# Gram's attention, its query block: three product banks, one bank pair for turning, totals a tile ahead, copies by ScalarE alone, first contexts normalised between the tiles

## The chip, the cores and the metric

The kernel runs on one core of a Trainium2 chip. The metric is the device time of one execution in microseconds. TensorE is the matrix engine, VectorE (DVE) and ScalarE (ACT) are the two that read its results from PSUM, GpSimd (POOL) works on SBUF alone here, and SyncE (SP) issues the transfers.

## The reference

Four layers of gated cross-attention and feed-forward over 32 sequences of 56 tokens of width 128, each attending to a context of 1500 rows. The change is in the attention of the third layer (`L2_xattn`), 16 heads of 64, which has no softmax:

```python
Qn = _layernorm(Q, ln1_g, ln1_b)
Kn = _layernorm(K, ln1_g, ln1_b)
Vn = _layernorm(V, ln1_g, ln1_b)
q = _split_heads(Qn @ wq, B, Nq)
k = _split_heads(Kn @ wk, B, Nk)
v = _split_heads(Vn @ wv, B, Nk)
qn = _l2norm(q)      # q / max(sqrt(sum(q * q)), 1e-12), per head
kn = _l2norm(k)
attn = jnp.einsum('bhqd,bhkd->bhqk', qn, kn)
out = jnp.einsum('bhqk,bhkd->bhqd', attn, v)
x = Q + out @ wo + bo
```

Since nothing nonlinear stands between the two products, the kernel never forms `attn`: it sums a Gram matrix of normalised keys and contexts for each sequence and multiplies the queries into it.

## The kernel before

`attention2` computes this layer with queues written out by hand: each engine has its list of instructions, in the order of the code, and semaphores between them. It has three blocks with a barrier between each. The block `attn2q`, the one that changes, makes the normalised queries of all 1792 tokens, in 16 tiles (`TILES`) of 112 tokens (`PAIR`, two sequences). The block `attn2k` behind it goes over the 32 sequences with their contexts, in 12 chunks of 125 rows (`CH`, `KC`); it needs the queries, turned, and the first sequence's context, normalised. The block `attn2m` is the layer's small network.

In `attn2q`, TensorE first multiplies the value and output weights of each head (`vo`, into the two product banks `pq[0]` and `pq[1]`, each two PSUM banks of 512 columns); ScalarE copies them to `w_vo`. Each tile t then goes these ways:

- *query*: TensorE, two products of 512 columns each (L2282; each shows as two passes in the trace), into `pq[t % 2]`;
- *square*: ScalarE, 112x1024, into `q_sq` (L2306);
- *total*: VectorE sums the squares by head (L2327); *root*: ScalarE (L2309);
- *clip* and *reciprocal*: VectorE, 112x16 (L2332, L2333); then `qn`: VectorE scales the product bank by them (L2335), which also frees the bank;
- *turning*: TensorE transposes `qn` in eight pieces (L2273) into `pt[t % 2]`, a pair of PSUM banks; *copy*: ScalarE takes one bank (L2300), VectorE the other (L2323), into `q_t`.

TensorE's queue goes query(0), query(1), turning(0), query(2), turning(1) and so on. Query(t) waits for `qn`(t-2), because of its bank. ScalarE's goes square(t), root(t), copy(t-1); VectorE's total(t), copy(t-1), clip(t), reciprocal(t), `qn`(t).

The first sequence's context is normalised beside this: its statistics by VectorE ahead of tile 0 (`context_stats`, `context_scales`), a root by ScalarE (`context_root`, L2229), the twelve chunks by ScalarE (`context_normed`, L2235), gain and shift by GpSimd over all twelve in two instructions (`context_affine`, L2240 and L2243), which wait for the last chunk. For the other sequences the same happens in `attn2k`.

All eight PSUM banks are taken in this block: four by `pq`, four by `pt`.

## Time and profile before

| | us |
|---|---|
| median of three runs | 6049.69 |
| lowest, highest | 6029.98, 6051.38 |
| profiled execution, its time | 6069.86 |
| profiled execution, its span | 6067.9 |
| TensorE busy in it | 5280.6 (87%) |
| VectorE busy | 4463.5 (74%) |
| ScalarE busy | 3193.1 (53%) |
| GpSimd busy | 1846.4 (30%) |
| mean granted TensorE clock | 0.94 of 2.4 GHz |

The span is from the first to the last instruction of the execution that was profiled; its time is 2 us more. All rows below are of this one execution, and times in them count from its start. Busy time is that of an engine's own instructions. A row in order of time gives the start, the duration, the engine and the line, then output, inputs and shapes; behind it in brackets stands how long the engine had been idle and what ended that.

### The profile page before, as it was taken

What the parts mean: (1) busy time and instruction counts of PE and PEld (TensorE: products, weight loads), DVE (VectorE), ACT (ScalarE), POOL (GpSimd) and SP (SyncE); (2) the same over time, 40 slices, a digit from 0 to 9 for tenths busy, and PEclk for the clock granted to TensorE, in tenths of its full rate; (3) what the DMA queues carried; (4) which work ended last, traced back from release to release, by engine and by line L of the source; (5) the groups of instructions that cost most, each with busy time, mean ns of one, the idle gap of its engine ahead of it and who ended that gap; (6) DMA issues with size and microseconds to landing.
All of it is one profiled execution on the core that took longest, in us unless ns stands there. A gap on an engine that the chain in (4) does not pass through costs nothing. (4 is left out here: it accounts for less than half of the span.)

```text
span 6067.9 us, 133226 instructions
## 1 busy us (share of the span) xinstructions
PE 5280.6 (87%) x51447; PEld 3803.5 (63%) x51447; DVE 4463.5 (74%) x9176; ACT 3193.1 (53%) x6024; POOL 1846.4 (30%) x1447
## 2 busy tenths in 40 slices
PE   3898898988679999987949999999999749999997
PEld 1777777777268887865924444444444427878885
DVE  7888888886367777762457777777777557777776
ACT  1666666666256666642224444444444326666663
POOL 5776767672122222202021111111111022222220
PEclk6999999999789999988979999999999879999998
DMA  5655555553267777742010000000000049888891
GB/s 126 132 122 131 126 128 126 126 128 80 51 128 140 139 135 142 141 84 101 22 33 26 16 15 15 15 15 15 15 15 10 8 101 156 159 163 162 161 156 28
DMA packets 369568, 545.00 MB, mean 90 GB/s; under 512 B 116084, under 2 KB 248310, under 8 KB 368806
## 3 DMA queue, kind: packets, MB, share of 16 engines
q1 hardware_dynamic: 366982, 533.81, 43.5%
q8 instruction: 380, 6.23, 0.5%
q0 software_dynamic: 2048, 3.67, 0.2%
q14 instruction: 158, 1.29, 0.1%
HBM read 413.45 MB, written 123.90 MB: 89 GB/s over the span
## 5 line engine op out<-in xcount | busy, mean ns | idle before, releaser
L698 DVE CUSTOM_DVE_ANT_0 attn_logits<-attn_scores,attn_shift 112x750 f32<-112x750 f32 x1024 | 945.8, 933 | 436.5 <-PE attn_scores L503 436.5
L616 ACT ACTIVATE attn_probs_t<-attn_pt 125x448 f32<-125x448 f32 x1536 | 829.4, 541 | 583.7 <-PE attn_pt L518 563.2
L518 PEld LDWEIGHTS attn_pt<-ident,attn_logits 112*125 112x125 f32 x6144 | 852.6, 189 | 180.0 <-issue 95.1
L518 PE MATMUL attn_pt<-ident,attn_logits 112*125 112x112 f32 x6144 | 921.4, 273 | 26.7 <-ACT attn_logits L607 23.8
L2385 PE MATMUL attn2k_pk<-attn_wk,attn_cn_t 128*125 128x512 f32 x1536 | 740.1, 604 | 39.8 <-ACT attn_cn_t L2451 36.6
L2396 PE MATMUL attn2k_pg<-attn_kn,attn_cn 125*128 125x512 f32 x1536 | 726.2, 595 | 4.5 <-ACT attn_gram L2459 2.3
L2504 DVE TENSOR_REDUCE attn_ss<-attn_sq 125x16 f32<-125x1024 f32 x384 | 467.0, 1216 | 245.3 <-ACT attn_sq L2478 245.0
L415 POOL CAST attn_k_parts<-xn_t 128x500 bf16<-128x500 f32 x192 | 206.3, 1075 | 1429.2 <-DVE xn_t L670 1429.2
L2478 ACT ACTIVATE attn_sq<-attn2k_pk 125x1024 f32<-125x1024 f32 x384 | 391.5, 1019 | 330.8 <-PE attn2k_pk L2385 330.6
L1230 ACT ACTIVATE attn_probs_t<-attn_pt 125x448 f32<-125x448 f32 x768 | 413.9, 539 | 278.2 <-PE attn_pt L1117 276.3
L2385 PEld LDWEIGHTS attn2k_pk<-attn_wk,attn_cn_t 128*125 128x125 f32 x1536 | 274.7, 187 | 400.6 <-issue 298.3
L503 PE MATMUL attn_scores<-attn_k_packed,attn_q_blocks 96*112 96x375 bf16 x2048 | 515.2, 333 | 9.9 <-DMA attn_k_packed<-k_scratch 8.2
L2516 DVE TENSOR_TENSOR attn_kn<-attn2k_pk,attn_rn 125x1024 f32<-125x1024 f32 x384 | 470.2, 1224 | 13.4 <-DVE attn_rn L2513 0.2
L1105 PE MATMUL attn_scores<-attn_k_packed,attn_q_blocks 96*112 96x375 bf16 x1024 | 353.3, 345 | 125.6 <-DVE attn_tops L1411 125.5
L2396 PEld LDWEIGHTS attn2k_pg<-attn_kn,attn_cn 125*128 125x128 f32 x1536 | 264.6, 192 | 299.0 <-issue 287.2
L1411 DVE CUSTOM_DVE_ANT_0 attn_logits<-attn_scores,attn_bias,attn_floor 112x750 f32<-112x750 f32 x342 | 338.2, 989 | 96.9 <-PE attn_scores L1107 95.2
L2367 POOL COPY attn_q_now<-attn_q_t 128x448 f32 (+1 forms) x32 | 17.8, 556 | 1194.2 <-PE attn2k_pz L2417 1135.3
L1219 ACT ACTIVATE attn_logits<-attn_logits,attn_neg_top 112x750 f32<-112x750 f32 x342 | 313.1, 916 | 102.3 <-DVE attn_neg_top L1419 100.1
L607 ACT ACTIVATE attn_logits<-attn_logits,attn_neg_top 112x750 f32<-112x750 f32 x384 | 351.3, 915 | 3.9 <-DVE attn_neg_top L706 0.6
L531 PE MATMUL attn_po<-attn_probs_t,attn_v 125*32 125x112 f32 x12288 | 347.9, 261 | 1.5 <-ACT attn_probs_t L616 1.3
L1107 PE MATMUL attn_scores<-attn_masked,attn_pusher 112*112 112x375 bf16 x1024 | 341.3, 333 | 0.0
L452 PE MATMUL attn_side<-attn_ctx_t,attn_wk 128*128 128x500 f32 x376 | 207.8, 635 | 147.1 <-DVE xn_t L670 77.1
(371 smaller groups left out, 10444.3 us busy)
## 6 DMA issues: line engine op xcount, KB each, us to landing
attn_k_packed<-k_scratch SPq DMA_DIRECT2D x372, 375.0 KB
attn_k_packed<-k_scratch SPq DMA_DIRECT2D x408, 187.5 KB, 4.4
k_scratch<-attn_k_parts SPq DMA_DIRECT2D x64, 1125.0 KB
attn_ctx_t<-in_ctx_t SPq DMA_DIRECT2D x64, 750.0 KB
k_scratch<-attn_k_parts SPq DMA_DIRECT2D x96, 375.0 KB, 3.7
attn_ctx_t<-in_ctx_t SPq DMA_DIRECT2D x96, 250.0 KB, 4.6
attn_ctx<-in_ctx SPq DMA_DIRECT2D x32, 750.0 KB
attn_mask_in<-in_mask SPq DMA_DIRECT2D x192, 109.4 KB
```

What stands on the lines that cost most here:

```text
L503: last = pe.matmul(scores[h][0:PAIR, b, 0:QTR], q_blocks[:, n % 2, p, :, :].rearrange("p a s -> p (a s)"), k_packed[:, n % 2, p, h * HALF ...
L518: last = pe.transpose(pt[(3 * at + t) % 2][0:KC, (c % 4) * PAIR:(c % 4 + 1) * PAIR], logits[:, at % 3, c * KC:(c + 1) * KC], g.ident[0:PAI ...
L607: act.activation(at, at, ACT.Identity, bias=neg_top[:, n % 2, p:p + 1]).then_inc(act_lowered, 1)
L616: act.activation(probs_t[0:KC, p // 4, 4 * t:4 * t + 4, (p % 4) * PAIR:(p % 4 + 1) * PAIR], pt[(3 * at + t) % 2][0:KC, 0:QUAD].rearrange(" ...
L698: dve.tensor_tensor_reduce(out=logits[:, at % 3, cols].rearrange("p (b k) -> p b k", b=2), in0=scores[h][0:PAIR, :, 0:QTR], in1=shift[:, n ...
L1105: pe.matmul(scores[h][0:PAIR, b, 0:QTR], q_blocks[:, n % 2, p, :, :].rearrange("p a s -> p (a s)"), k_packed[:, at % KEY_RING, cols], star ...
L1230: act.activation(probs_t[0:KC, at % PV_RING, 4 * t:4 * t + 4, :], pt[(3 * at + t) % 2][0:KC, 0:QUAD].rearrange("p (c q) -> p c q", c=4), A ...
L2385: last = pe.matmul(pk[c % 2][0:KC, b, :], cn_t[:, c % 2, :], wk[:, b * HW:(b + 1) * HW], start=True, stop=True)
L2396: last = pe.matmul(pg[:, b, :], cn[:, j, c, :], kn[:, c % 2, b * HW:(b + 1) * HW], start=(c == 0), stop=(c == CH - 1))
L2478: act.activation(sq[:, c % 2, :].rearrange("p (a b) -> p a b", a=2), pk[c % 2][0:KC, :, :], ACT.Square).then_inc(sq_ready, 1)
L2504: dve.tensor_reduce(ss[:, c % 2, :], sq[:, c % 2, :].rearrange("p (h d) -> p h d", h=H2), AX.X, ALU.add).then_inc(ss_ready, 1)
L2516: dve.tensor_tensor(kn[:, c % 2, :].rearrange("p (h d) -> p h d", h=H2), pk[c % 2][0:KC, :, :].rearrange("p a (h d) -> p (a h) d", h=8), r ...
```

## The change

Three pairs of PSUM banks for products instead of two, and one pair for turning instead of two. TensorE makes three queries ahead and then, behind the turning of tile t, the query of tile t+3; a turning waits for the copy of the tile before. ScalarE copies the weights first, works on squares two tiles and roots one tile ahead, copies both banks of a turned tile in one instruction, and normalises one chunk of the first context behind each of the copies 0 to 11. VectorE copies nothing and makes the total of a tile before it normalises the tile ahead of it.

```diff
--- before.py
+++ after.py
@@ -2245,11 +2245,11 @@
 
         r = scope(nc, "attn2q")
         with r.ctx:
-            pq = [r.ps(f"pq{i}", [128, 2, 512]) for i in range(2)]
-            pt = [r.ps(f"pt{i}", [128, 2, 512]) for i in range(2)]
-            vo_ready, vo_copied, q_ready, q_sq_ready, q_ss_ready, q_root_ready, q_steps, qn_ready, q_turned, act_copied, dve_copied = (
+            pq = [r.ps(f"pq{i}", [128, 2, 512]) for i in range(3)]
+            pt = r.ps("pt", [128, 2, 512])
+            vo_ready, vo_copied, q_ready, q_sq_ready, q_ss_ready, q_root_ready, q_steps, qn_ready, q_turned, copied = (
                 r.sem(n) for n in ("vo_ready", "vo_copied", "q_ready", "sq_ready", "ss_ready",
-                                   "root_ready", "steps", "qn_ready", "q_turned", "act_copied", "dve_copied"))
+                                   "root_ready", "steps", "qn_ready", "q_turned", "copied"))
             with nc.Block() as block:
                 @block.gpsimd
                 def _(pool):
@@ -2267,49 +2267,62 @@
 
                     def turn(t):
                         pe.wait_ge(qn_ready, t + 1)
-                        wait(pe, act_copied, t - 1)
-                        wait(pe, dve_copied, t - 1)
+                        wait(pe, copied, t)
                         for p in range(HP):
-                            last = pe.transpose(pt[t % 2][:, p // 4, (p % 4) * PAIR:(p % 4 + 1) * PAIR],
+                            last = pe.transpose(pt[:, p // 4, (p % 4) * PAIR:(p % 4 + 1) * PAIR],
                                                 qn[:, t % 2, p * 128:(p + 1) * 128], g.ident[0:PAIR, 0:PAIR])
                         last.then_inc(q_turned, 1)
 
-                    for t in range(TILES):
+                    def query(t):
                         if t < 2:
                             pe.wait_ge(vo_copied, t + 1)
-                        wait(pe, qn_ready, t - 1)
+                        wait(pe, qn_ready, t - 2)
                         for c in range(2):
-                            last = pe.matmul(pq[t % 2][0:PAIR, c, :], g.z_t[:, t * PAIR:(t + 1) * PAIR],
+                            last = pe.matmul(pq[t % 3][0:PAIR, c, :], g.z_t[:, t * PAIR:(t + 1) * PAIR],
                                              wq[:, c * HW:(c + 1) * HW], start=True, stop=True)
                         last.then_inc(q_ready, 1)
-                        if t:
-                            turn(t - 1)
-                    turn(TILES - 1)
+
+                    for t in range(3):
+                        query(t)
+                    for t in range(TILES):
+                        turn(t)
+                        if t + 3 < TILES:
+                            query(t + 3)
 
                 @block.scalar
                 def _(act):
-                    context_root(act, 0)
-                    context_normed(act, 0, 0, range(CH))
                     for half in range(2):
                         act.wait_ge(vo_ready, half + 1)
                         act.activation(w_vo[:, 8 * half:8 * half + 8, :].rearrange("p h d -> p (h d)"),
                                        pq[half][:].rearrange("p a b -> p (a b)"), ACT.Copy).then_inc(vo_copied, 1)
 
+                    def square(t):
+                        act.wait_ge(q_ready, t + 1)
+                        wait(act, q_ss_ready, t - 1)
+                        act.activation(q_sq[:, t % 2, :].rearrange("p (a b) -> p a b", a=2), pq[t % 3][0:PAIR, :, :],
+                                       ACT.Square).then_inc(q_sq_ready, 1)
+
+                    def root(t):
+                        act.wait_ge(q_ss_ready, t + 1)
+                        act.activation(q_ss[:, t % 2, :], q_ss[:, t % 2, :], ACT.Sqrt).then_inc(q_root_ready, 1)
+
                     def copy(t):
                         act.wait_ge(q_turned, t + 1)
-                        act.activation(q_t[:, 0:4, t * PAIR:(t + 1) * PAIR],
-                                       pt[t % 2][:, 0, 0:QUAD].rearrange("p (a b) -> p a b", a=4),
-                                       ACT.Copy).then_inc(act_copied, 1)
+                        act.activation(q_t[:, :, t * PAIR:(t + 1) * PAIR].rearrange("p (g a) b -> p g a b", g=2),
+                                       pt[:, :, 0:QUAD].rearrange("p g (a b) -> p g a b", a=4),
+                                       ACT.Copy).then_inc(copied, 1)
+                    context_root(act, 0)
+                    square(0)
+                    square(1)
+                    root(0)
                     for t in range(TILES):
-                        act.wait_ge(q_ready, t + 1)
-                        wait(act, q_ss_ready, t - 1)
-                        act.activation(q_sq[:, t % 2, :].rearrange("p (a b) -> p a b", a=2), pq[t % 2][0:PAIR, :, :],
-                                       ACT.Square).then_inc(q_sq_ready, 1)
-                        act.wait_ge(q_ss_ready, t + 1)
-                        act.activation(q_ss[:, t % 2, :], q_ss[:, t % 2, :], ACT.Sqrt).then_inc(q_root_ready, 1)
-                        if t:
-                            copy(t - 1)
-                    copy(TILES - 1)
+                        if t + 2 < TILES:
+                            square(t + 2)
+                        if t + 1 < TILES:
+                            root(t + 1)
+                        copy(t)
+                        if t < CH:
+                            context_normed(act, 0, 0, (t,))
 
                 @block.vector
                 def _(dve):
@@ -2318,25 +2331,23 @@
                     context_scales(dve, 0)
                     chain = Chain(dve, q_steps)
 
-                    def copy(t):
-                        dve.wait_ge(q_turned, t + 1)
-                        dve.tensor_copy(q_t[:, 4:8, t * PAIR:(t + 1) * PAIR],
-                                        pt[t % 2][:, 1, 0:QUAD].rearrange("p (a b) -> p a b", a=4)).then_inc(dve_copied, 1)
-                    for t in range(TILES):
+                    def total(t):
                         dve.wait_ge(q_sq_ready, t + 1)
                         dve.tensor_reduce(q_ss[:, t % 2, :], q_sq[:, t % 2, :].rearrange("p (h d) -> p h d", h=H2),
                                           AX.X, ALU.add).then_inc(q_ss_ready, 1)
-                        if t:
-                            copy(t - 1)
+
+                    total(0)
+                    for t in range(TILES):
+                        if t + 1 < TILES:
+                            total(t + 1)
                         dve.wait_ge(q_root_ready, t + 1)
                         chain(dve.tensor_scalar(q_rn[:, t % 2, :], q_ss[:, t % 2, :], 1e-12, None, ALU.max))
                         chain(dve.reciprocal(q_rn[:, t % 2, :], q_rn[:, t % 2, :]))
                         wait(dve, q_turned, t - 1)
                         dve.tensor_tensor(qn[:, t % 2, :].rearrange("p (h d) -> p h d", h=H2),
-                                          pq[t % 2][0:PAIR, :, :].rearrange("p a (h d) -> p (a h) d", h=8),
+                                          pq[t % 3][0:PAIR, :, :].rearrange("p a (h d) -> p (a h) d", h=8),
                                           q_rn[:, t % 2, :].unsqueeze(2).broadcast_to((PAIR, H2, DH2)),
                                           ALU.mult).then_inc(qn_ready, 1)
-                    copy(TILES - 1)
 
         r = scope(nc, "attn2k")
         with r.ctx:
```

The first place is TensorE's queue from the block's start. `attn2q_pq` are the product banks, `attn2q_pt` the banks for turning; L2264 makes the weight products, `x4` are two queries of two instructions each. Before:

```order
L2259 UNCONDITIONAL_BRANCH
L2264 MATMUL attn2q_pq<-attn_wo,attn_wv_t 128x128 x16
L2282 MATMUL attn2q_pq<-attn_wq,z_t 112x512 x4
L2273 MATMUL attn2q_pt<-ident,attn_q_qn 128x112 x8
L2282 MATMUL attn2q_pq<-attn_wq,z_t 112x512 x2
```

And now:

```order
L2259 UNCONDITIONAL_BRANCH
L2264 MATMUL attn2q_pq<-attn_wo,attn_wv_t 128x128 x16
L2281 MATMUL attn2q_pq<-attn_wq,z_t 112x512 x6
L2272 MATMUL attn2q_pt<-ident,attn_q_qn 128x112 x8
L2281 MATMUL attn2q_pq<-attn_wq,z_t 112x512 x2
```

Three queries instead of two stand ahead of the first turning; from there on one turning and one query alternate in both.

The second place is ScalarE's queue from the block's start. Before:

```order
L2229 ACTIVATE attn_var<-attn_var 125x12
L2235 ACTIVATE attn_cn<-attn_ctx,attn_off,attn_rs 125x128 x12
L2295 ACTIVATE attn_w_vo<-attn2q_pq 128x1024 x2
L2306 ACTIVATE attn_q_sq<-attn2q_pq 112x1024
L2309 ACTIVATE attn_q_ss<-attn_q_ss 112x16
L2306 ACTIVATE attn_q_sq<-attn2q_pq 112x1024
L2309 ACTIVATE attn_q_ss<-attn_q_ss 112x16
L2300 ACTIVATE attn_q_t<-attn2q_pt 128x4x112
```

And now:

```order
L2296 ACTIVATE attn_w_vo<-attn2q_pq 128x1024 x2
L2229 ACTIVATE attn_var<-attn_var 125x12
L2302 ACTIVATE attn_q_sq<-attn2q_pq 112x1024 x2
L2307 ACTIVATE attn_q_ss<-attn_q_ss 112x16
L2302 ACTIVATE attn_q_sq<-attn2q_pq 112x1024
L2307 ACTIVATE attn_q_ss<-attn_q_ss 112x16
L2311 ACTIVATE attn_q_t<-attn2q_pt 128x8x112
L2235 ACTIVATE attn_cn<-attn_ctx,attn_off,attn_rs 125x128
```

The weight copies (`attn_w_vo`) moved ahead of everything, the twelve contexts (`attn_cn`) stand one by one behind the copies of tiles 0 to 11, squares run two tiles ahead and roots one, and a copy takes all eight pairs of heads.

The third place is VectorE's queue at its first tiles, behind the statistics of the first sequence. Before:

```order
L2327 TENSOR_REDUCE attn_q_ss<-attn_q_sq 112x16
L2332 TENSOR_SCALAR attn_q_rn<-attn_q_ss 112x16
L2333 RECIPROCAL attn_q_rn<-attn_q_rn 112x16
L2335 TENSOR_TENSOR attn_q_qn<-attn2q_pq,attn_q_rn 112x1024
L2327 TENSOR_REDUCE attn_q_ss<-attn_q_sq 112x16
L2323 COPY attn_q_t<-attn2q_pt 128x4x112
L2332 TENSOR_SCALAR attn_q_rn<-attn_q_ss 112x16
```

And now:

```order
L2336 TENSOR_REDUCE attn_q_ss<-attn_q_sq 112x16 x2
L2344 TENSOR_SCALAR attn_q_rn<-attn_q_ss 112x16
L2345 RECIPROCAL attn_q_rn<-attn_q_rn 112x16
L2347 TENSOR_TENSOR attn_q_qn<-attn2q_pq,attn_q_rn 112x1024
L2336 TENSOR_REDUCE attn_q_ss<-attn_q_sq 112x16
```

The copy is gone from this queue, and between two normalisations stands the total of the tile after the next one (before: of the next one).

## Rows read from the trace of the kernel before

**Rows 1.** The page, its first lines: span, and busy time of the engines.
```profile
span 6067.9 us, 133226 instructions
...
PE 5280.6 (87%) x51447; PEld 3803.5 (63%) x51447; DVE 4463.5 (74%) x9176; ACT 3193.1 (53%) x6024; POOL 1846.4 (30%) x1447
```

**Rows 2.** Windows: stretch, length, busy PE, PEld, DVE, ACT, POOL, clock, DMA, GB/s.
```profile
3126.60:3182.80 56.20, 40.75 (x181) 20.30 (x179) 49.96 (x75) 25.55 (x45) 2.84 (x1) 1.00 0.00 1
3182.80:3185.00 2.20, 0.00 (x0) 0.00 (x0) 2.13 (x5) 0.65 (x2) 0.00 (x0) 0.86 0.00 0
3185.00:3188.00 3.00, 1.75 (x8) 1.41 (x8) 0.69 (x2) 0.54 (x1) 0.00 (x0) 0.50 0.00 0
3188.00:3200.00 12.00, 8.41 (x11) 2.95 (x11) 3.68 (x9) 2.87 (x6) 0.55 (x1) 0.58 0.30 91
```

**Rows 3.** Waits in 3123 to 3188: who for whom, us, times, longest.
```profile
PE attn2q_pt L2273 <- DVE attn_q_qn L2335: 17.8, 16, 2.7
DVE attn_q_ss L2327 <- ACT attn_q_sq L2306: 13.9, 8, 10.3
ACT attn_q_sq L2306 <- PE attn2q_pq L2282: 11.9, 15, 2.7
```

**Rows 4.** Order of time, two tiles and the end: start, duration, engine.
```profile
3177.89 0.99 PE L2273 MATMUL attn2q_pt<-ident,attn_q_qn 112*128 112x112 f32 x8 [0.63 <-DVE attn_q_qn L2335]
...
3178.71 1.88 PE L2282 MATMUL attn2q_pq<-attn_wq,z_t 128*112 128x512 f32 x4
...
3180.51 1.22 DVE L2335 TENSOR_TENSOR attn_q_qn<-attn2q_pq,attn_q_rn 112x1024 f32<-112x1024 f32 x1
3180.63 1.02 ACT L2306 ACTIVATE attn_q_sq<-attn2q_pq 112x1024 f32<-112x1024 f32 x1 [0.38 <-PE attn2q_pq L2282]
3181.69 1.22 DVE L2327 TENSOR_REDUCE attn_q_ss<-attn_q_sq 112x16 f32<-112x1024 f32 x1
...
3182.82 0.61 DVE L2323 COPY attn_q_t<-attn2q_pt 128x448 f32<-128x448 f32 x1
3182.94 0.21 ACT L2309 ACTIVATE attn_q_ss<-attn_q_ss 112x16 f32<-112x16 f32 x1 [1.29 <-DVE attn_q_ss L2327]
...
3183.35 0.17 DVE L2332 TENSOR_SCALAR attn_q_rn<-attn_q_ss 112x16 f32<-112x16 f32 x1
...
3183.84 1.23 DVE L2335 TENSOR_TENSOR attn_q_qn<-attn2q_pq,attn_q_rn 112x1024 f32<-112x1024 f32 x1
...
3185.12 1.75 PE L2273 MATMUL attn2q_pt<-ident,attn_q_qn 112*128 112x112 f32 x8 [2.35 <-DVE attn_q_qn L2335]
...
3186.91 0.63 DVE L2323 COPY attn_q_t<-attn2q_pt 128x448 f32<-128x448 f32 x1 [1.85 <-PE attn2q_pt L2273]
```

**Rows 5.** Order of time at the block's start.
```profile
3113.21 7.16 PE L2264 MATMUL attn2q_pq<-attn_wo,attn_wv_t 64*128 64x128 f32 x32 [1.82 <-PEq L105]
...
3117.63 4.72 ACT L2235 ACTIVATE attn_cn<-attn_ctx,attn_off,attn_rs 125x128 f32<-125x128 f32 x12 [0.50 <-DVE attn_off L2225]
3122.26 1.91 ACT L2295 ACTIVATE attn_w_vo<-attn2q_pq 128x1024 f32<-128x1024 f32 x2
...
3123.31 5.18 PE L2282 MATMUL attn2q_pq<-attn_wq,z_t 128*112 128x512 f32 x8 [2.94 <-ACT attn_w_vo L2295]
...
3126.82 1.02 ACT L2306 ACTIVATE attn_q_sq<-attn2q_pq 112x1024 f32<-112x1024 f32 x1 [2.65 <-PE attn2q_pq L2282]
...
3129.87 1.22 DVE L2335 TENSOR_TENSOR attn_q_qn<-attn2q_pq,attn_q_rn 112x1024 f32<-112x1024 f32 x1
```

**Rows 6.** Groups in 3120 to 3188: ScalarE's copy of a turned half.
```profile
L2300 ACT ACTIVATE attn_q_t<-attn2q_pt 128x448 f32<-128x448 f32 x16 | 8.4, 526 | 3.3 <-PE attn2q_pt L2273 3.3
```

**Rows 7.** The block behind: GpSimd and VectorE in time, and line 2511.
```profile
3229.12 3.44 POOL L2240 TENSOR_TENSOR attn_cn<-attn_cn,attn_gain 125x1536 f32<-125x1536 f32 x1 [40.25 <-ACT attn_cn L2235]
...
3231.48 1.11 DVE L2511 TENSOR_SCALAR attn_rn<-attn_ss 125x16 f32<-125x16 f32 x1 [0.28 <-ACT attn_ss L2483]
...
L2511 DVE TENSOR_SCALAR attn_rn<-attn_ss x384: 155/175/1112, 3198.3 to 4757.1; 125x16 f32<-125x16 f32 x192
```

## The prediction

> **What bounds the kernel now.** I began with the page: TensorE is busy for 87% of a span of 6067.9 us, VectorE for 74% [rows 1]. Those are averages over eight layers, and the change touches one block of one layer, so I went on to the table of windows around that block. It runs from 3113.2 to 3187.5 us: some 74 us, 1.2% of the span. In the stretch 3126.60 to 3182.80 VectorE is busy for 49.96 of 56.20 us and TensorE for 40.75, at a granted clock of 1.00 (2.4 GHz) [rows 2]. So VectorE is nearly, not wholly, the bound, and the waits say why. VectorE's `total` waits for ScalarE's `square` eight times, in every other tile; `square` waits for the query product in 15 tiles; TensorE's turning waits 17.8 us in all for `qn` [rows 3]. (10.3 of VectorE's 13.9 us is the first wait, ahead of tile 0.) A ring of three engines sets the pace.
>
> The order of time gives the ring's length [rows 4]. From the start of one turning to that of the next but one, start to start: turning to query 0.82 us; query to square 1.92; square to total 1.06; total to VectorE's copy 1.13; copy to clip 0.53; clip to `qn`, with the reciprocal between, 0.49; `qn` to turning 1.28. Sum 7.23, and that is what lies between the first and the last of these rows (3177.89 to 3185.12) for two tiles. The query behind the turning of tile t is that of tile t+2, hence two tiles a lap: 3.62 us a tile.
>
> **The change, part by part.**
>
> VectorE's copy goes. It stands in the ring with 0.53. The new ring is: turn(t), then query(t+3), square(t+3), total(t+3), and since totals are now a tile ahead, total(t+3) stands directly before clip(t+2), `qn`(t+2), which turn(t+2) waits for. The third product bank lets the query run three tiles ahead, but the total, a tile ahead too, takes that tile back: a lap is still two tiles. Its length is 0.82 + 1.92 + 1.06 + 1.13 + 0.49 + 1.28 = 6.70 us, 3.35 a tile. The root of tile t+2 was taken a tile earlier, so clip doesn't wait for it. VectorE by itself needs 1.13 + 0.49 + 1.18 (`qn` to the next total, 3180.51 to 3181.69 [rows 4]) = 2.80, so tiles come by turns after 2.80 and 3.90 us. From `qn`(0) to `qn`(14) there are seven laps, 46.90 us. `qn`(15) has no total ahead of it and follows 1.18 + 0.49 = 1.67 us later: 48.57. Before, it took from 3129.87 [rows 5] to 3183.84 [rows 4], 53.97. **Gain 5.4.**
>
> ScalarE's copy grows from 448 to 896 columns. 448 take 0.526 us [rows 6], two of 1024 columns take 1.91 [rows 5], about 1.00 each, so 896 take between 0.53 and 1.05 (twice the half copy). I take 0.90, the line between 526 and 1003 ns. With one bank for turning, turn(t+1) waits for copy(t): turning 0.98, copy 0.90 and two hops of 0.04 make 1.96 us after the turning began, and the next `qn` is ready 2.80 after it at the earliest. So the lost second bank costs nothing while TensorE has its fast clock; 0.84 us of cover is left. ScalarE's other work in a tile: square 1.02 and root 0.21 [rows 4], one context 0.39 (12 in 4.72 [rows 5]); with the copy 2.5 of at least 2.80. The context stands behind the copy: turning to end of copy 1.96, plus 0.39 is 2.35, and the next square can start only 0.82 + 1.92 = 2.74 after the turning. It hides, with 0.4 to spare; without that cover it would cost its 12 x 0.39 = 4.7.
>
> The head. Before, ScalarE normalises 12 contexts (4.72) ahead of the two weight copies, and TensorE's query waits for them until 3123.31, though its products ended at 3120.37 [rows 5]. Now the first weight copy starts when its products are there, the second from 3120.41 to 3121.4 under query(0), so query(0) starts at about 3120.40. The eight passes of the first two queries take 5.18 with the clock as it then rises [rows 5]; I keep 5.18, so square(1) starts at 3125.62. `qn`(0) now stands behind total(1): + 1.06 + 1.13 + 0.49 = 3128.30. **Gain 1.57** against 3129.87: of the 2.9 us that the query starts earlier, the second tile's total takes 1.3 back.
>
> The tail. `qn`(15) starts at 3128.30 + 48.57 = 3176.87, `qn`(14) at 3175.20, turn(14) at 3176.48. TensorE's last query is now behind turn(12), so before turn(14) it has been idle for some 2.9 us. Before, the granted clock was 0.86 in the 2.20 us stretch ahead of the last turning and 0.50 in the one that holds it, and that turning took 1.75 us instead of 0.98 [rows 2, 4]. I give turn(14) and turn(15) 1.75 each: turn(14) to 3178.23, copy 0.90, turn(15) 3179.2 to 3180.97, copy to 3181.90. That is 5.03 after `qn`(15) began, where before it was 3.70 (3183.84 to 3187.54). **Loss 1.33.**
>
> GpSimd's two instructions on the contexts (3.44 us each) move from the head, where VectorE had nothing to do, to the middle of the loop: context 11 is done at about 3168.2, so they lie at 3168.4 to 3171.8 and 3171.9 to 3175.3, 6 us before the block's end. They are hidden from the next block, but not from VectorE: while a GpSimd instruction ran from 3229.12 to 3232.56, a small TENSOR_SCALAR of VectorE started at 3231.48 and took 1.11 us, to that very end; the median of 384 of them is 175 ns [rows 7]. clip is such an instruction. clip(13), due at 3170.8, would be held to 3171.8, which the 1.10 us of slack before the next long tile absorbs; clip(14), due at 3174.7, to 3175.3, less its own 0.17. **Loss 0.4.** The Trainium skill says so too ("SBUF — State Buffer", section "Who interferes with whom"): the two engines share a port pair, locked for the whole instruction, which a tensor_scalar can take and a tensor_reduce never does; by that rule the hold is the whole rest of GpSimd's instruction. By this rule, the trace agrees (1.11 us, to the instruction's end), and taken alone it allows two full holds, 6.5 us.
>
> Sum: 5.40 + 1.57 - 1.33 - 0.4 = 5.2 us. The profiled execution (6069.86) would become 6064.7; it lies 20 us above the median of the three runs, 6049.69, but the block's waits are a matter of engines and hold for both, so I take the difference off the median: **6044.5**. What comes behind the block is unchanged and merely starts earlier: its 12 us under a clock of 0.58 [rows 2] follow an idle TensorE before and now. That is the largest unknown: with 8.41 us of products in it, a full clock would save 4.2, and a stay at half speed as much longer would cost about 4.
>
> **The rivals.**
>
> *VectorE sets the pace* (0.08). If squares come early enough in each tile, only 2.80 a tile is left: 14 x 2.80 + 1.67 = 40.9 instead of 48.57, and 6037. For it: the third bank. Against it: the query is still issued behind the turning that waits for `qn`.
>
> *The loop's gain is eaten* (0.17). Place: VectorE's clip under GpSimd's pass over the contexts. Two full holds cost 2 x (3.44 - 0.17) = 6.5, giving 6050.7. For it: the hold in [rows 7]. Against it: the clips are due late in GpSimd's instructions, and half of it falls into slack. The same time comes out if the contexts do not hide on ScalarE (4.7, 6049). It would decide from a hold of 5 us on.
>
> *Slower: TensorE runs the loop at half clock* (0.05). A query then takes 3.47 (that of tile 0, 3123.31 to the square's 3126.82 [rows 5]) and a turning 1.75, 5.22 a tile on TensorE alone: from 3120.4 on 83.5 and a copy, to 3204.8 instead of 3187.5, so 17 us slower, 6067. It decides if the idle before a turning in the loop grows from 1.2 us to the length that went ahead of the fall at the end, near 2. In the new ring it is 3.90 - 2.70 (0.82 and the query's 1.88) = 1.20 at most, as now, so I don't expect it.
>
> **How the numbers follow.** 30 us are what this kernel's measurement tells from no change (0.5%), 40% of the whole block; no case here reaches it. Forecast 0.70 (6044.5, with its unknowns 6040 to 6049), rivals 0.30; what lies beyond all is the program's own scatter, 21 us over three runs. Range: 6037 on the near side and 6051 on the far one, each carried 6 to 11 us further for that scatter of a median: 6026 to 6057. Faster by over 0.5% 0.03, within 0.5% 0.94, slower 0.03.
>
> **What would show it.** In the profile after: `qn` starts by turns 2.8 and 3.9 us apart (steps of 2.8 throughout: the first rival; near 5: the third); VectorE waits for square in every other tile, about 1.1 us; the first query starts within 0.1 us of the last weight product; ScalarE's 896 columns near 0.90; one or two clips of 0.5 to 1.1 us; the last two turnings at 1.75; the block ends near 69 us after its first product instead of 74.3. The prediction is wrong if the block gains over 10 us or nothing, or if the next block's first 12 us change length.

## The result: slower by 0.56%

The changed kernel takes 6075.71 us (median of 6 runs, 6071.14 to 6088.99), the kernel before 6047.57 in its six. The ratio is 1.0056, with a 95% interval of 1.0039 to 1.0074: slower, where no change that can be measured was forecast, and 19 us beyond the far end of the range.

The profiled execution took 6088.99 us. Its page has these lines for [rows 1]:

```profile
span 6087.1 us, 133211 instructions
PE 5304.3 (87%) x51447; PEld 3808.0 (63%) x51447; DVE 4456.8 (73%) x9160; ACT 3200.4 (53%) x6024; POOL 1847.6 (30%) x1447
q14 instruction: 223, 1.83, 0.1%
```

The last line had no part in the prediction; in the page of before it reads:

```profile
q14 instruction: 158, 1.29, 0.1%
```

The queue that brings the engines' code moves 65 packets of 8 KB more, for a program that is 15 instructions shorter (16 fewer of VectorE, one more of TensorE).

**The query block is faster.** This is the changed kernel in order of time: the block's first product, the first queries and `qn`s, two turns of the loop, and the end.

```profile
3096.15 7.16 PE L2264 MATMUL attn2q_pq<-attn_wo,attn_wv_t 64*128 64x128 f32 x32 [1.81 <-PEq L105]
...
3103.24 7.72 PE L2281 MATMUL attn2q_pq<-attn_wq,z_t 128*112 128x512 f32 x12
...
3109.28 1.02 ACT L2302 ACTIVATE attn_q_sq<-attn2q_pq 112x1024 f32<-112x1024 f32 x1 [1.23 <-PE attn2q_pq L2281]
...
3111.96 1.22 DVE L2347 TENSOR_TENSOR attn_q_qn<-attn2q_pq,attn_q_rn 112x1024 f32<-112x1024 f32 x1
...
3114.27 0.92 ACT L2311 ACTIVATE attn_q_t<-attn2q_pt 128x896 f32<-128x896 f32 x1 [2.14 <-PE attn2q_pt L2272]
...
3114.72 1.23 DVE L2347 TENSOR_TENSOR attn_q_qn<-attn2q_pq,attn_q_rn 112x1024 f32<-112x1024 f32 x1
...
3117.05 1.22 DVE L2336 TENSOR_REDUCE attn_q_ss<-attn_q_sq 112x16 f32<-112x1024 f32 x1 [1.11 <-ACT attn_q_sq L2302]
...
3118.67 1.22 DVE L2347 TENSOR_TENSOR attn_q_qn<-attn2q_pq,attn_q_rn 112x1024 f32<-112x1024 f32 x1
...
3121.43 1.23 DVE L2347 TENSOR_TENSOR attn_q_qn<-attn2q_pq,attn_q_rn 112x1024 f32<-112x1024 f32 x1
...
3152.12 3.44 POOL L2240 TENSOR_TENSOR attn_cn<-attn_cn,attn_gain 125x1536 f32<-125x1536 f32 x1 [90.77 <-ACT attn_cn L2235]
...
3154.59 1.01 DVE L2344 TENSOR_SCALAR attn_q_rn<-attn_q_ss 112x16 f32<-112x16 f32 x1
...
3155.65 3.44 POOL L2243 TENSOR_TENSOR attn_cn<-attn_cn,attn_shift 125x1536 f32<-125x1536 f32 x1
...
3158.39 0.73 DVE L2344 TENSOR_SCALAR attn_q_rn<-attn_q_ss 112x16 f32<-112x16 f32 x1
...
3160.72 1.76 PE L2272 MATMUL attn2q_pt<-ident,attn_q_qn 112*128 112x112 f32 x8 [2.54 <-DVE attn_q_qn L2347]
...
3161.07 1.22 DVE L2347 TENSOR_TENSOR attn_q_qn<-attn2q_pq,attn_q_rn 112x1024 f32<-112x1024 f32 x1
...
3165.34 0.92 ACT L2311 ACTIVATE attn_q_t<-attn2q_pt 128x896 f32<-128x896 f32 x1 [1.91 <-PE attn2q_pt L2272]
```

`qn` starts by turns 2.76 and 3.95 us apart (3111.96, 3114.72, 3118.67, 3121.43). From the first product to the last copy's end it is 3166.26 - 3096.15 = 70.1 us, against 3187.54 - 3113.21 = 74.3 [rows 4, 5]: 4.2 us less, where 5.2 were forecast.

**The block behind it is slower.** Here every key product of the following block (`attn2k_pk`) as one group, first in the kernel before, then in the changed one; the last two times are the first and the last start:

```profile
L2385 PE MATMUL attn2k_pk<-attn_wk,attn_cn_t x1536: 590/592/1218, 3189.1 to 4753.9; 128*125 128x512 f32 x192
```

```profile
L2396 PE MATMUL attn2k_pk<-attn_wk,attn_cn_t x1536: 590/592/1216, 3167.8 to 4774.7; 128*125 128x512 f32 x192
```

1564.8 us have become 1606.9. The same products are made by the same lines, and their durations are the same; 42.1 us have come in between them. The waits of the changed kernel from 3167 to 4779 us name the place:

```profile
DVE attn_ss L2515 <- ACT attn_sq L2489: 230.3, 238, 10.4
...
DVE attn_ss L2515 <- issue: 55.5, 13, 4.6
```

"Issue" is time in which an engine waited for nothing that the profile shows. Before, VectorE has no such wait in this stretch. There are 13 of 4.1 to 4.6 us, and each stands at the same place: where VectorE's hardware loop over the sequences (`sequences`, 14 passes of two sequences each) jumps back to its start. One in VectorE's order of time, then the same place in the kernel before:

```profile
3466.70 1.23 DVE L2527 TENSOR_TENSOR attn_kn<-attn2k_pk,attn_rn 125x1024 f32<-125x1024 f32 x1
3472.05 1.22 DVE L2515 TENSOR_REDUCE attn_ss<-attn_sq 125x16 f32<-125x1024 f32 x1 [4.13 <-issue]
3473.19 0.86 DVE L2207 BATCH_NORM_STATS2 attn_stats<-attn_ctx 125x6 f32<-125x128 f32 x4
```

```profile
3484.30 1.23 DVE L2516 TENSOR_TENSOR attn_kn<-attn2k_pk,attn_rn 125x1024 f32<-125x1024 f32 x1
3487.36 1.22 DVE L2504 TENSOR_REDUCE attn_ss<-attn_sq 125x16 f32<-125x1024 f32 x1 [1.84 <-ACT attn_sq L2478]
3488.50 0.86 DVE L2207 BATCH_NORM_STATS2 attn_stats<-attn_ctx 125x6 f32<-125x128 f32 x4
```

Before, the pause is 1.84 us and ends with ScalarE's square. After, it is 4.13, nothing in the program ends it, and a pass takes 101.2 us on average instead of 98.0. In the 7 us around it (3466 to 3473) the only transfers in the whole core are these:

```profile
DMA packets 3, 0.02 MB, mean 4 GB/s; under 512 B 0, under 2 KB 0, under 8 KB 0
## 3 DMA queue, kind: packets, MB, share of 16 engines
q14 instruction: 3, 0.02, 1.2%
```

Three packets of code, the first just as the normalisation ends, the next two 2.4 us apart. 65 packets more are 13 times 5: five for each repeated pass.

The spans add up. Ahead of the query block the changed kernel's profile is 17.1 us shorter (3096.15 against 3113.21), in code that the change leaves alone. What makes that difference was not settled: some waits there are shorter (VectorE's for `ffn_silu`, 158.7 us against 177.9), others longer (for `ffn_py`, 74.0 against 57.4). Over the kernels below the query block begins at 3079 to 3132 us, and the repeated times of one kernel spread over 15 to 32 us. Then -4.2 in the query block, +42.1 in the key products, -1.6 behind them: +19.2, the difference of the spans (6087.1 and 6067.9). Of the medians' 28 us, the two blocks give +38; the rest is within that scatter.

### The profile page after: what moved, and what is told of

It reads as the page before. It is cut to its first block and busy times, and to the rows that moved or that the text cites. A ratio compares the mean times of both kernels' runs of the same rounds, so it can differ in the third digit from the quotient of the medians.

```text
span 6087.1 us, 133211 instructions
## 1 busy us (share of the span) xinstructions
PE 5304.3 (87%) x51447; PEld 3808.0 (63%) x51447; DVE 4456.8 (73%) x9160; ACT 3200.4 (53%) x6024; POOL 1847.6 (30%) x1447
## 5 line engine op out<-in xcount | busy, mean ns | idle before, releaser
L2515 DVE TENSOR_REDUCE attn_ss<-attn_sq 125x16 f32<-125x1024 f32 x384 | 467.1, 1216 | 287.6 <-ACT attn_sq L2489 230.3
L2494 ACT ACTIVATE attn_ss<-attn_ss 125x16 f32<-125x16 f32 x384 | 82.8, 216 | 511.4 <-DVE attn_ss L2515 511.4
```

What stands on the lines that cost most here:

```text
L2515: dve.tensor_reduce(ss[:, c % 2, :], sq[:, c % 2, :].rearrange("p (h d) -> p h d", h=H2), AX.X, ALU.add).then_inc(ss_ready, 1)
```

## The experiments

What could make VectorE fetch code in its loop? Counted in the built program, its stream has 9777 instructions before and 9761 after (the 16 copies are gone), and the loop's body, 288 instructions long, starts at number 6757 before and 6741 after. The four streams other than TensorE's hold 20388 instructions before; over 158 packets that is 129 for a packet of 8 KB. If code lies in pieces of 128, as this suggests, a body of 288 lies in three pieces, unless it starts in the last 31 places of one; then it lies in four. That is the **theory of place**: sixteen instructions fewer ahead of the loop moved its head to the end of a piece. Its rivals: the **new order** of the query block leaves engines or data in a state that slows what follows; or the **execution** itself, a disturbance that would come with any program.

Most kernels here differ from the changed one by one edit, in `attention2`, with N and the place varied. The increments are of a semaphore that nobody waits for, and leave the computation as it is:

```
                         qn(t)
+                    for _ in range(N):
+                        dve.sem_inc(held, 1)
```

**pad16**: N = 16, behind the last `qn` of the query block. It keeps all that the change does and puts the loop's head back to where it was.

> The changed kernel with 16 semaphore increments of VectorE, which nobody waits for, behind its last qn in the query block. They change nothing but the place of what follows in VectorE's instruction stream: the loop of 14 passes in the block behind stands where it stood in the kernel before (the change took 16 copies out of that stream ahead of it). Theory P (place of the code): the 13 stalls of 4.1 to 4.6 us at the head of VectorE's loop body go, as do the 65 extra packets of the instruction queue (158 packets again), the block behind takes 1568 us again instead of 1611, and the kernel takes 6043 +- 6 us, 0.1% under the kernel before; the query block stays at 70 us. Theory B (the block's new order puts the engines into another step with each other, and the loop behind runs slower for it): the increments change no order, so the stalls stay and the time stays at 6076. Theory D (the slow loop is a matter of the execution, not of the program): times of both kinds, 6043 and 6080, among the runs.

Ratio to the kernel before 0.9993 (0.9976 to 1.0009), and on its page and in its trace:

```profile
q14 instruction: 158, 1.29, 0.1%
```

```profile
L2398 PE MATMUL attn2k_pk<-attn_wk,attn_cn_t x1536: 590/592/1217, 3182.2 to 4745.6; 128*125 128x512 f32 x192
```

1563.4 us for the key products, no wait on "issue" in VectorE, and a query block of 70.8 us. Sixteen instructions more take the loss away.

**pad16_behind**: the same sixteen, put behind VectorE's loop.

> The same 16 increments, but behind VectorE's loop instead of ahead of it. Theory P: the loop stands where it stands in the changed kernel, so nothing is cured: 13 stalls, 223 packets of the instruction queue, 6076 +- 6 us. Theory B: 6076 as well. If some 16 increments anywhere cure it (the length of the program, not the loop's place), 6043.

1.0045 (1.0032 to 1.0058); 223 packets, 13 waits on "issue" (54.4 us in all), key products 1601.0 us. It has as many instructions as pad16, and the median is 33 us longer (6099.51 and 6066.28, on one chip). So it is what stands ahead of the loop that counts.

**act_copies**: the kernel before, in its old order, with only the copies given to ScalarE. VectorE's stream is shorter by the same sixteen.

```
-                        wait(pe, dve_copied, t - 1)
...
-                        act.activation(q_t[:, 0:4, t * PAIR:(t + 1) * PAIR],
-                                       pt[t % 2][:, 0, 0:QUAD].rearrange("p (a b) -> p a b", a=4),
+                        act.activation(q_t[:, :, t * PAIR:(t + 1) * PAIR].rearrange("p (g a) b -> p g a b", g=2),
+                                       pt[t % 2][:, :, 0:QUAD].rearrange("p g (a b) -> p g a b", a=4),
...
-                        if t:
-                            copy(t - 1)
...
-                    copy(TILES - 1)
```

> The kernel before with one part of the change alone: ScalarE copies both halves of a turned tile (896 columns), VectorE none; two product banks, two for turning, the old order of everything else. VectorE's stream ahead of the loop loses the same 16 instructions as in the changed kernel. Theory P: the stalls appear here too, 13 of them with 223 packets of the instruction queue, the block behind takes 1611 us; the query block itself becomes 1 us faster (total to clip now 1.48 us with the root in it instead of 1.66: 7.05 us a lap instead of 7.23), so 6047 - 1 + 42 = 6085 by the profiles, and 6075 to 6085 in time. Theory B: the order that could matter (three product banks, one for turning, contexts late) is not there, so 6046.

1.0057 (1.0040 to 1.0074); 223 packets, 13 waits (53.9 us), key products 1601.7. The old order has the whole loss. Its query block takes 73.1 us, 1.2 less than before.

**total_behind_qn**: pad16 with `total(t+1)` moved behind `qn(t)`, so that nothing that waits for ScalarE's square stands ahead of a `qn` that is ready. It has pad16's sixteen increments too.

```
-                        if t + 1 < TILES:
-                            total(t + 1)
...
                         qn(t)
+                        if t + 1 < TILES:
+                            total(t + 1)
```

> pad16 with VectorE's total of tile t+1 moved behind the qn of tile t (it stood ahead of clip of tile t). Theory ring (the total, a tile ahead, takes back the tile that the third product bank gives): a lap is now three tiles and no longer binds, VectorE alone does: 0.49 + 1.18 + 1.48 (total, then the root, which it must now wait for) = 3.15 us a tile, steps all alike instead of 2.8 and 3.9 by turns; qn(0) to qn(15) 47.3 instead of 49.1 us; no wait for square. Rival: the wait for the root costs as much as the wait for square did: 3.35 a tile. Either way the kernel's time differs from pad16 by 2 us, which only the profile tells; 6041 +- 6 by theory P, 6074 if the stalls stay.

0.9980 (0.9966 to 0.9994), the lowest ratio of all versions here. VectorE no longer waits for the square in the loop, but a little for the root:

```profile
DVE attn_q_rn L2342 <- ACT attn_q_ss L2307: 4.8, 16, 0.6
```

```profile
3143.35 1.23 DVE L2345 TENSOR_TENSOR attn_q_qn<-attn2q_pq,attn_q_rn 112x1024 f32<-112x1024 f32 x1
...
3146.48 1.22 DVE L2345 TENSOR_TENSOR attn_q_qn<-attn2q_pq,attn_q_rn 112x1024 f32<-112x1024 f32 x1
...
3149.61 1.22 DVE L2345 TENSOR_TENSOR attn_q_qn<-attn2q_pq,attn_q_rn 112x1024 f32<-112x1024 f32 x1
```

Every step is 3.13 us long, where 2.8 and 3.9 by turns make 3.35. The block takes 67.0 us: `qn`(0) to `qn`(15) 48.8 us (47.3 expected), about as in the changed kernel, because GpSimd's two instructions now hold clips for 1.65 and 0.56 us with no slack to absorb it, and 3 us less at the two ends (`qn`(0) 14.3 us after the block's start, and 4.0 from `qn`(15) to the last copy's end, where it was 15.8 and 5.2). Against pad16, from which it differs by this edit alone, the block is 3.8 us shorter, and 1.7 of that is one overlong step of pad16's loop, which the clock makes (see the head's paragraph below) and which does not occur here. The median is 15 us under that of before, of which the query block explains 7; I take the rest for scatter.

**ctx_ahead**: pad16 with the twelve contexts normalised ahead of the weight copies again.

> pad16 with one part undone: ScalarE normalises the twelve contexts ahead of the weight copies, as before. By the steps of the profiles: contexts ready 9.1 us after the block's start, second weight copy's end and query(0) at about 10.1, square(1) 6.0 later, total(1), clip, qn(0) 2.7 later: qn(0) 18.8 us after the first weight product instead of 15.8, so 3.0 later; GpSimd's passes lie in the head again, so no clip is held (it was 1.01 and 0.73 us, of which 0.5 to 1 us reached the end). Net 2 to 2.5 us longer than pad16 from the first weight product to the last copy (70 to 72.3). Rival: it costs nothing, since the loop is bound elsewhere.

Its block takes 73.5 us, 2.7 more than pad16's; no clip is held (166 ns at most); `qn`(0) comes 18.3 us after the block's start. 158 packets, key products 1564.3. So moving the contexts is worth 2.7 us, the holds included, more than half of what the block gains. Each of the two blocks was profiled once, and both have that overlong step.

**pad128, pad96, pad8**: how large is a piece? If 128 instructions, 128 increments bring the loss back; if 256, they don't.

> pad16 with 128 increments instead of 16 ahead of VectorE's loop. In the changed kernel each of the 13 later passes fetches five packets of 8 KB, and all packets of the queue outside the loop make one for every 128 instructions of VectorE, ScalarE, GpSimd and SyncE together (20388 instructions, 158 packets). Theory P128: code is held in pieces of 128 instructions, and only the loop's place within a piece matters; 128 more move it by one whole piece, to the same place as in the changed kernel, so the 13 stalls and the 65 packets (plus one for the longer program) are back: 224 packets, block behind 1605 us. Rival P256: pieces of 256; the loop then stands half a piece on, in two pieces, and there is no stall: 159 packets, 1566 us. Theory B (pads near the loop disturb its step) has no reason for stalls with 128 and none with 16.

> 96 increments instead of 16. VectorE's loop body has 288 instructions: in pieces of 128 it lies in four if it starts in the last 31 places of one, otherwise in three. The change moved it 16 places back and into a stall, so it now starts in one of the last 16 places; 96 more put it in the middle of the next piece: no stall, some 158 packets, block behind 1566 us. With pieces of 256 also no stall; it serves with pad128 to tell a length of 128 from 'many increments bring the stalls'. If more increments than some number always stall: 13 stalls here as well.

> 8 increments instead of 16. The border between stall and none lies between 0 and 16 places on; by theory P this run can only show all 13 stalls (223 packets) or none (158), nothing between: the border is a place in the stream, not a slope. A cost that grew with the distance moved would show some 2 us a pass instead of 4.

pad128 has 224 packets, 55.2 us of waits on "issue", and key products of 1607.8 us. pad96 has 159 packets, no such wait and 1564.9; pad8 158, none and 1566.0. The loss comes back after 128 places. These three and ctx_ahead were timed once each, beside one run of the kernel before (6074.70 us): 6131.44, 6069.71, 6066.74 and 6067.80. One run says nothing below the scatter, so the counts and the key products carry the argument; only pad128 stands out in time as well.

**pad112, before_pad104**: both heads lie in the last 31 places of a piece, but not at its very end; the second is the kernel before with 104 increments behind its last copy.

> 112 increments: 16 places short of a whole piece of 128 beyond the changed kernel. So far 0 and 128 stall, 8, 16 and 96 don't. If a stall means that the loop body of 288 instructions lies in four pieces of 128, the stretch of places that stall is 31 long and ends between 0 and 7; then 112 (16 before 128) is in it: 13 stalls, 224 packets or 223. Rival: only a body that starts in the last few places of a piece stalls, say 8, since what is fetched ahead at the jump is what matters; then none, 159 packets.

> The kernel before, whole, with 104 increments behind VectorE's last copy in the query block: its loop then stands 16 + 104 = 120 places beyond that of the changed kernel, 8 places short of a whole piece. Theory P: nothing of the change is in this kernel, and it stalls all the same: 13 stalls of 4 us, some 224 packets, block behind 1605 us instead of 1565; the increments themselves cost about 60 ns each, 6 us, ahead of the barrier. Theory B: 1565 us, as in the kernel before.

Half a miss each. Both have the 224 packets, and neither has the long waits: key products 1572.6 us with no wait on "issue", and 1571.7 with six, of 1.6 us together. So four pieces are fetched again in each pass, as expected, but that costs only 5 to 9 us; something else makes it 40. (Timed once each: 6040.91 and 6060.50 us, the kernel before 6040.83. The second also has its 104 increments ahead of the barrier, some 9 us.)

**pad2, pad124**: where is the border? Two increments, the smallest edit that the waits allow (VectorE stands at the body's third instruction, so at most two lie ahead of the border), and 124, which leave 5 or 6 places ahead of the border.

> 2 increments ahead of VectorE's loop. The changed kernel waits at the third instruction of the loop's body, and the kernel before with 104 increments, whose body starts 8 places earlier, waits 0.16 us at the tenth: both put the border between two pieces of 128 one or two places behind the body's start in the changed kernel. Then 2 places more bring the body wholly behind the border, into three pieces: 158 packets, no stall, block behind 1565 us, and a ratio to the kernel before of 0.999, where the changed kernel has 1.0056. Rival: the border is 3 to 7 places on (all that the runs with 8 increments and none show), then 223 packets and 13 stalls.

> 124 increments: the body starts 4 places earlier than in the changed kernel (one whole piece on), so 5 or 6 places ahead of a border. The body lies in four pieces, so five packets a pass and 224 in all by every theory. What is open is the wait: with 1 or 2 places it is 4 us at the jump, with 9 and 17 places almost nothing though the same packets are fetched. If a long wait needs the border within the first few instructions of the body (before the first that takes time), then it is there with 2 and gone with 5: block behind 1572 us. If it shrinks with the places left, some of the 3.3 us a pass remains: 1580 to 1600 us.

pad2: 0.9988 (0.9976 to 0.9999), 158 packets, key products 1565.5. Two increments take the whole loss away. pad124 (timed once, 6054.04 us): 224 packets, key products 1581.5 us, and the wait has moved to the next instruction and shrunk:

```profile
DVE attn_stats L2207 <- issue: 12.8, 13, 1.2
```

One of its jumps in order of time:

```profile
3453.79 1.23 DVE L2529 TENSOR_TENSOR attn_kn<-attn2k_pk,attn_rn 125x1024 f32<-125x1024 f32 x1
3456.86 1.22 DVE L2517 TENSOR_REDUCE attn_ss<-attn_sq 125x16 f32<-125x1024 f32 x1 [1.84 <-ACT attn_sq L2491]
3459.24 0.87 DVE L2207 BATCH_NORM_STATS2 attn_stats<-attn_ctx 125x6 f32<-125x128 f32 x4 [1.16 <-issue]
```

The total, ahead of the border, starts 1.84 us after the normalisation's end, just as in the kernel before; the statistics, behind the border, start 4.2 us after it, about when the changed kernel's total did (4.13). So what the border costs is a time after the jump, and work that lies ahead of the border is done within it.

Together, by the places that lie between the head of VectorE's loop and the next border (the border is 1 or 2 places behind the head in the changed kernel, since two increments pass it):

| places left | kernels | packets | waits on "issue" | key products, us |
|---|---|---|---|---|
| 1 or 2 | changed, act_copies, pad16_behind, pad128 | 223, 224 | 13 of 4.1 to 4.7 us | 1601.0 to 1607.8 |
| 5 or 6 | pad124 | 224 | 13 of about 1 us | 1581.5 |
| 9 or 10 | before_pad104 | 224 | 6, 1.6 us in all | 1571.7 |
| 17 or 18 | pad112 | 224 | none | 1572.6 |
| over 31 | before, pad2, pad8, pad16, pad96, ctx_ahead, total_behind_qn | 158, 159 | none | 1563.4 to 1566.5 |

## Why the prediction was wrong

**The step that failed** is "What comes behind the block is unchanged and merely starts earlier". Its products and its order were unchanged; the place of its loop in VectorE's code was not. Sixteen copies gone ahead of the loop moved its 288 instructions from three pieces of 128 into four, with one or two of them in the first. They are then fetched anew in each pass, and VectorE stands still for 4.1 to 4.6 us each time it jumps back. The prediction put that block at a difference of nothing; it measured +42.1 us. I had an eye on the clock in that block's first 12 us as its one unknown; they did not change (a clock of 0.60 and 8.14 us of products, against 0.58 and 8.41 [rows 2]). Place is shown from both sides: the changed kernel loses its loss with 2, 8, 16 or 96 instructions more ahead of the loop, keeps it with 16 behind, gets it back with 128; and the old order with sixteen fewer has all of it. The new order and the execution are both ruled out by that.

Why 13 stalls of about 4.3 us, 55.5 in all, cost 42 and not 55: VectorE waits less for the square in turn, 230.3 us in 238 waits instead of 245.0 in 258. At the jump itself it would have waited 1.84 us anyway, and behind the pause it is late for squares that are then ready. 55.5 less 14.7 is 41, and 13 times 3.2, the growth of a pass, is 42.

That a body in three pieces stays and one in four doesn't would fit a store of four pieces, with one always being fetched ahead, hence five packets in a pass; the counts agree with it, and no run tests it otherwise. The Trainium skill has notes on it ("Advanced Engine Details and Errata", section "ISA Cache", and "Runtime: NRT & Kernel Launch", section "Instruction fetch mechanics"): 32 KB for an engine other than TensorE, lines of 16 KB with 256 instructions, and an engine that waits when it jumps to code outside the window. The 32 KB agree with four pieces of 8 KB, and so does the wait at the jump. The 256 don't: by them the loss would come back after 256 places, and with a line always fetched ahead a body of 288 would be fetched again in every pass wherever it stood; here the border repeats after 128, and before, it is fetched once. The first of the two sections says that the line's size can be set for each engine, so VectorE's may simply be another here; no run shows the setting.

Why the wait shrinks as more instructions lie ahead of the border can be read from the traces. In the changed kernel, pad124, before_pad104 and pad112 alike a packet moves within 0.2 us of the end of a pass's last normalisation and the next 2.4 to 2.9 us behind it. The first instruction behind the border starts 3.95 to 4.6 us after that end wherever it comes before the engine has other work: the total in the changed kernel (4.1 to 4.6), the statistics in pad124 (3.95 to 4.3), the clip in before_pad104 (3.98 to 4.35, against 3.75 without the border). In pad112 the border lies behind the next normalisation, which itself starts only at 4.2 to 4.5, so nothing waits. That the pause is two fetches one behind the other, first the head's piece and then the next, is argued from this, not tested; how the engine chooses what to fetch, no run here shows.

**The loop's gain, 5.40 less 0.4**: right in this execution. `qn`(0) to `qn`(15) took 49.1 us instead of 53.97, 4.9 less. The steps were 2.76 and 3.95 (2.80 and 3.90 forecast), the wait for the square about 1.1, the copy of 896 columns 0.92 (0.90), and nothing waits for the single turning bank. It held in pad2 as well (49.1). In the eight other kernels whose TensorE works in this order and whose totals stand ahead of the clips, pad16 among them, the loop took 50.2 to 50.8, for the reason in the paragraph on the head.

**GpSimd's hold**: right in kind and about right in size. Clips took 1.01 us at 3154.59, to just behind the end of GpSimd's instruction (3155.56), and 0.73 at 3158.39.

**The head, 1.57**: the mechanism is right, the term was 0.85 in this execution: `qn`(0) came 15.81 us after the block's start instead of 16.66. The query did start at once (3103.24), but square(1) came 6.04 us behind it and not 5.22. That duration hangs on when TensorE's clock rises, and over the kernels with three queries ahead it is 4.9 to 6.4 us. An early rise isn't kept, though: in pad16 square(1) came after 5.09 us and `qn`(0) 14.9 after the block's start, but TensorE, idle for 2.28 us ahead of its first turning, then ran three microseconds at its lower level (1.2 GHz):

```profile
3127.00:3130.00 3.00, 3.00 (x6) 1.16 (x5) 1.56 (x4) 1.30 (x2) 0.00 (x0) 0.51 0.02 5
```

The third number from the end, 0.51, is the granted clock. The changed kernel has the same idle there and kept the full clock. pad16's next long step took 5.64 us instead of 3.95, by a wait of 2.79 for the square. That is the third rival's mechanism, in one lap: it turns the head's larger gain into a block of 70.8 us instead of 70.1. It is the rule and not the exception: of the ten kernels profiled with this idle of 2.28 us, eight (pad16, pad16_behind, pad8, pad96, pad112, pad124, pad128, ctx_ahead) have such a step of 5.3 to 5.6 us. Only the changed kernel and pad2 have not, the two in which square(1) had come last (6.0 and 6.4 us behind the query, at most 5.8 in the others). What I called a fixed duration hangs on the clock, and each kernel was profiled once, so how often either outcome comes in one kernel is open.

**The tail, 1.33**: 1.49. TensorE stood 2.54 us ahead of turn(14), and the last two turnings took 1.76 and 1.73 (1.75 each forecast), so the clock was at its lower level for both.

**The rivals**: none came true. VectorE alone does not set the pace, the gain was not eaten inside the block, TensorE did not run the loop at half clock (beyond the one lap in eight of the kernels). The case that did come, a loss in code that isn't touched, was not among them; the 0.03 for a slower kernel was not meant for it.

## What to carry to other kernels

Adding or removing instructions moves all that stands behind them on that engine; where a hardware loop follows, look at the instruction queue's packets on the page before and after, and at waits on "issue" at the loop's head. When such a count grows with the passes, put a few instructions that do nothing ahead of the loop and time that, before judging the change: here 2 of them turned 1.0056 into 0.9988. And when an edit touches 1% of the span and the time moves more than that part could give, measure the length of each untouched block first.

## What the runs showed of the hardware

- VectorE's code comes in packets of 8 KB, and the border between two pieces repeats after 128 instructions. A loop body of 288 instructions in three such pieces is fetched once; one in four costs five packets in each pass.
- The wait this makes depends on how many of the body's instructions stand ahead of the first border: 4.1 to 4.7 us with one or two, about 1 with five or six, next to nothing from nine on, though the packets stay. The first instruction behind the border starts no sooner than some 4 us after the jump (3.95 to 4.6).
- Increments used as filler cost VectorE some 0.1 us each once there are many: from 96 to 128 of them, the time between the query block's last copy and the first turning behind it grows from 4.9 to 8.0 us; in the changed kernel it is 0.8. In before_pad104, where they stand behind the last copy, 104 make it 10.2. Two cost nothing that these runs can show.
- Behind the same idle of 2.28 us of TensorE the clock fell in eight kernels (0.56 to 0.70 over the 3 us from the first turning) and held in two (1.00), with the same instructions around it. In total_behind_qn the idle there was 1.26 us, and the clock held.
